# Wide attention: scores from query weights multiplied into the keys, values folded pass by pass

## The reference

```
query = layernorm(x)                              # (8, 256, 128)
q = (query @ Wq + bq).reshape(b, sq, 16, 64)      # Wq: 128 x 1024
k = (key @ Wk + bk).reshape(b, 64, 16, 64)        # key = value = context
v = (value @ Wv + bv).reshape(b, 64, 16, 64)
scores = einsum('bqhd,bkhd->bhqk', q, k) / 8
attn = softmax(scores, axis=-1)
out = einsum('bhqk,bkhd->bqhd', attn, v).reshape(b, sq, 1024)
out = out @ Wo + bo + query
return layernorm(out) * ln_gamma + ln_beta
```

## Time and profile before

| what | us |
|---|---|
| median of 3 runs | 1546.37 (1543.95 to 1548.54) |
| profiled execution, own time | 1538.79 |
| its span, first to last instruction | 1537.1 |
| PE busy in the span | 1341.4 (87%) |
| DVE, ACT, POOL busy | 1054.2 (69%), 936.5 (61%), 878.9 (57%) |
| mean granted TensorE clock, share of full | 0.941 |

### The profile page before, as it was taken

How to read it: one execution, slowest core, us unless ns; L and a number is a source line. 1 busy time by engine, 2 the same in 40 slices (tenths; PEclk the granted TensorE clock), 3 DMA queues, 4 the chain that set the end, 5 groups by cost and what they waited for, 6 DMA issues and landing times. The chain is left out here.

```text
span 1537.1 us, 25078 instructions
## 1 busy us (share of the span) xinstructions
PE 1341.4 (87%) x8116; PEld 1040.6 (68%) x8116; DVE 1054.2 (69%) x2126; ACT 936.5 (61%) x1435; POOL 878.9 (57%) x619
## 2 busy tenths in 40 slices
PE   9789999797888887789489999998898349999998
PEld 8767777465466666646368887885787338787786
DVE  5534444597699999889756666673666766666665
ACT  4467787553787876477246765556665327555554
POOL 4168888300899999532047776661345128666655
PEclk9689999898899999899689999999999769999999
DMA  6021110000000000030044435332000135443442
GB/s 250 1 63 43 42 48 27 2 2 1 1 1 1 1 0 0 26 142 2 1 136 127 127 123 178 129 124 113 2 1 1 55 78 130 122 130 123 129 120 86
DMA packets 51561, 103.31 MB, mean 67 GB/s; under 512 B 6248, under 2 KB 10928, under 8 KB 49936
## 3 DMA queue, kind: packets, MB, share of 16 engines
q1 hardware_dynamic: 51472, 102.17, 21.6%
HBM read 99.99 MB, written 2.16 MB: 66 GB/s over the span
## 5 line engine op out<-in xcount | busy, mean ns | idle before, releaser
L1541 POOL TENSOR_TENSOR RA<-RW 128x1024 f32<-128x1024 f32 x128 | 246.7, 1965 | 86.1 <-ACT RW L1502 86.1
L881 ACT ACTIVATE PS<-PS 128x512 f32<-128x512 f32 (+1 forms) x260 | 151.1, 582 | 215.3 <-PE PS L677 214.6
L974 POOL TENSOR_TENSOR l3f_hid_rest<-RW,l3f_hid_high 128x512 fp32r<-128x512 f32 x132 | 170.5, 1292 | 141.3 <-ACT l3f_hid_high L873 141.3
L974 POOL TENSOR_TENSOR l2f_hid_rest<-RW,l2f_hid_high 128x512 fp32r<-128x512 f32 x128 | 165.3, 1292 | 136.9 <-ACT l2f_hid_high L873 136.9
L974 POOL TENSOR_TENSOR l0f_hid_rest<-RW,l0f_hid_high 128x512 fp32r<-128x512 f32 x128 | 165.2, 1292 | 64.7 <-ACT l0f_hid_high L873 56.4
L934 DVE TENSOR_TENSOR RW<-RW,PS 128x512 f32<-128x512 f32 (+1 forms) x260 | 178.7, 687 | 11.7 <-DVE RW L929 0.9
L1572 PE MATMUL PS<-identf,RA 128*128 128x128 f32 x1024 | 139.8, 287 | 37.0 <-DVE RA L1463 33.1
L1572 PEld LDWEIGHTS PS<-identf,RA 128*128 128x128 f32 x1024 | 118.1, 147 | 72.6 <-DVE RA L1463 69.3
L1463 DVE SCALAR_TENSOR_TENSOR RA<-RA,RW,PS 128x1024 f32<-128x1024 f32 x128 | 157.0, 1277 | 11.0 <-ACT PS L1508 10.4
L1508 ACT ACTIVATE PS<-RA 128x1024 f32<-128x1024 f32 x128 | 130.1, 1026 | 54.3 <-DVE RA L1463 51.8
L934 DVE TENSOR_TENSOR RW<-RD,PS 128x512 f32<-128x512 f32 x128 | 87.9, 687 | 108.3 <-ACT PS L881 99.9
(11 more groups left out here) (339 smaller groups left out, 3346.4 us busy)
## 6 DMA issues: line engine op xcount, KB each, us to landing
RD<-l2f_kept SPq DMA_DIRECT2D x128, 256.0 KB, 3.5
RB<-l3f_kept SPq DMA_DIRECT2D x128, 256.0 KB, 3.7
RD<-l0f_kept SPq DMA_DIRECT2D x32, 256.0 KB, 3.1
RA<-in_w SPq DMA_DIRECT2D x2, 2048.0 KB, 10.0
RA<-in_wg SPq DMA_DIRECT2D x2, 1024.0 KB, 9.7
RA<-in_wu SPq DMA_DIRECT2D x2, 1024.0 KB, 11.7
RA<-in_wd SPq DMA_DIRECT2D x2, 1024.0 KB, 13.6
RC<-in_wg SPq DMA_DIRECT2D x1, 2048.0 KB, 8.5
```

Source lines behind the costliest of these rows:

```text
L881: act.activation(gate, gate, e.func, bias=st.bias).then_inc(e.acted, 1)
L974: pool.tensor_tensor(rest, hid, high, ALU.subtract).then_inc(e.hidden_ready, 1)
L1541: pool.tensor_tensor(*pair_scores(r, h), ALU.add).then_inc(added, 1)
```

## The change

Queries are no longer made. Since a score is `(x Wq + bq) . k`, the query weights of a head are multiplied into its keys once: `M = Wq k`, 128 features by 64 context tokens for each head and batch, kept in `MK` (half of it in the place of `KT`, half where `QT` was). A score is then the product of `XT` and `M`. For the bias: a row of the layer norm sums to zero over its features, so feature 0 is minus the sum of the others. DVE subtracts column 0 of the query weights from the other columns and puts the bias `bq` in column 0 (`fold_queries`), and ACT stores `XT` with its row 0 set to the constant 1 (scale `rest`, bias from the identity's first column). The array `wq3` is laid out transposed on the host, with the same size.

The value products move behind the first scores. The folds become halves of a batch (`fold(n)`, 8 products instead of 16), of which two are made ahead of the loop and one in each of its first 14 passes. A fold writes the first 256 columns of banks 4 and 5, which are the banks of the turned weights too; ACT stores every fold (1850). The outputs use banks 6 and 7 in turn.

The core of the diff, without the declarations of semaphores:

```diff
+    VW_unit = RB[:, 8192:16384].rearrange("p (b h i f) -> p b i h f", b=B, h=2, i=2)
+    MK = [RA[:, 4096:8192].rearrange("p (c n) -> p c n", c=8), KT]
+    vw_ps, out_ps = PS[:, TURN:TURN + 2, 0:2 * D], [PS[:, OUT + r, 0:D] for r in range(2)]
...
         def _(dve):
+            def fold_queries():
+                dve.wait_ge(k.l3x_loaded, 64)
+                own.settle(dve.tensor_tensor(wq[:, :, 1:D], wq[:, :, 1:D], over(wq[:, :, 0], 2, D - 1),
+                                             ALU.subtract))
...
+                dve.tensor_copy(wq[:, :, 0], k.cols[:, at:at + 8]).then_inc(folded, 1)
+                dve.tensor_scalar(rest, k.identf[:, 0:1], -1.0, 1.0, ALU.mult, ALU.add).then_inc(rest_made, 1)
+            norm_vector(dve, k, nm, own, between=fold_queries)
+            for c in range(8):
+                dve.wait_ge(m_ready, c + 1)
+                dve.tensor_copy(MK[1][:, c, :], PS[:, 3 + 2 * (c % 2), :]).then_inc(m_stored[1], 1)
...
-                if t < 2:
-                    for b in ((1,), (3, 5, 7))[t]:
-                        dve.wait_ge(vw_ready, b + 1)
-                        dve.tensor_copy(VW[:, b].rearrange("p j d -> p (j d)"), vw_ps[1]).then_inc(vw_stored[1], 1)
...
         def _(act):
+            def store_m(c):
+                act.wait_ge(m_ready, c + 1)
+                act.activation(MK[0][:, c, :], PS[:, 2 + 2 * (c % 2), :], ACT.Copy).then_inc(m_stored[0], 1)
...
-                act.activation(k.XT[:, bass.ts(q, BLK)], PS[:, q, :], ACT.Copy).then_inc(nm.xt_ready, 1)
+                act.activation(k.XT[:, bass.ts(q, BLK)], PS[:, q, :], ACT.Identity, bias=k.identf[:, 0:1],
+                               scale=rest).then_inc(nm.xt_ready, 1)
...
+            for c in range(8):
+                store_v(c)
+                if c == 3:
                     exp(0)
             exp(1)
-            for j in range(JOBS):
-                store_q(1, j)
+            for n in range(2):
+                store_vw(n)
...
             for t in range(NT):
-                if t // 2 + 2 < B:
-                    for j in (2 * (t % 2), 2 * (t % 2) + 1):
-                        store_q(t // 2 + 2, j)
+                if t + 2 < 2 * B:
+                    store_vw(t + 2)
                 act.wait_ge(p_turned, t + 1)
...
         def _(pe):
+            def query_keys(c):
+                pe.wait_ge(k_stored, c + 1)
...
+                for h in range(2):
+                    rows = slice(64 * h, 64 * h + 64)
+                    mm = pe.matmul(PS[:, 2 + 2 * (c % 2) + h, :], wq[rows, c, :], KT[rows, c, :], start=True, stop=True)
+                mm.then_inc(m_ready, 1)
...
             def scores(t):
...
+                for h in range(2):
+                    mm = pe.matmul(score[t % 2][:, bass.ts(h, BLK)], k.XT[:, bass.ts(t, P)],
+                                   MK[h][:, :, bass.ts(t // 2, C)], start=True, stop=True)
...
+            def fold(n):
+                b, i = n // 2, n % 2
+                if n >= 1:
+                    pe.wait_ge(vw_stored, n)
+                if n >= 3:
+                    pe.wait_ge(p_stored, n - 2)
+                for jj in range(2):
                     for h in range(2):
                         for half in range(2):
...
             def output(t):
                 pe.wait_ge(p_stored, t + 1)
-                if t >= 1:
-                    pe.wait_ge(out_added, t)
+                if t >= 2:
+                    pe.wait_ge(out_added, t - 1)
...
+            pe.wait_ge(nm.xt_ready, 2)
+            scores(0)
             pe.wait_ge(nm.xt_ready, NB)
-            fold(0)
-            scores(0)
             scores(1)
...
+            for c in range(8):
+                value(c)
+            pe.wait_ge(v_stored, 8)
+            for n in range(2):
+                fold(n)
             for t in range(NT):
+                if t + 2 < 2 * B:
+                    fold(t + 2)
                 if t + 2 < NT:
                     scores(t + 2)
...
+                pe.wait_ge(vw_stored, min(t + 3, 2 * B))
                 turn(t)
```

More of the change, by code:

```diff
@@ L1815, in _, with store_v, store_vw @@
                                bias=k.col("bk3", c)).then_inc(k_stored, 1)
+                if c >= 1:
+                    store_m(c - 1)
+            store_m(7)
+            act.wait_ge(rest_made, 1)
             for q in range(NB):
                 act.wait_ge(nm.xt_turned, q + 1)
-                act.activation(k.XT[:, bass.ts(q, BLK)], PS[:, q, :], ACT.Copy).then_inc(nm.xt_ready, 1)
[L1820 to L1825, removed]
+                act.activation(k.XT[:, bass.ts(q, BLK)], PS[:, q, :], ACT.Identity, bias=k.identf[:, 0:1],
+                               scale=rest).then_inc(nm.xt_ready, 1)
+            def store_v(c):
+                act.wait_ge(v_ready, c + 1)
+                act.activation(VT[:, c, :], PS[:, 4 + c % 4, :], ACT.Identity,
+                               bias=k.col("bv3", c)).then_inc(v_stored, 1)
+            def store_vw(n):
+                act.wait_ge(vw_ready, n + 1)
+                act.activation(VW_unit[:, n // 2, n % 2], vw_ps, ACT.Copy).then_inc(vw_stored, 1)
             def exp(t):
@@ L1870, in _ @@
             pe.wait_ge(k.l3x_loaded, 64)
+            def query_keys(c):
+                pe.wait_ge(k_stored, c + 1)
+                if c == 0:
+                    pe.wait_ge(folded, 1)
+                if c >= 2:
+                    for m in range(2):
+                        pe.wait_ge(m_stored[m], c - 1)
+                for h in range(2):
+                    rows = slice(64 * h, 64 * h + 64)
+                    mm = pe.matmul(PS[:, 2 + 2 * (c % 2) + h, :], wq[rows, c, :], KT[rows, c, :], start=True, stop=True)
+                mm.then_inc(m_ready, 1)
             for c in range(8):
-                if c >= 2:
-                    pe.wait_ge(v_stored, c - 1)
-                pe.matmul(PS[:, 4 + c % 2, :], wv[:, c, :], k.ctxT[:], start=True, stop=True).then_inc(v_ready, 1)
                 if c >= 2:
@@ L1877, in _ @@
                 pe.matmul(PS[:, 6 + c % 2, :], wk[:, c, :], k.ctxT[:], start=True, stop=True).then_inc(k_ready, 1)
-            norm_tensor(pe, k, nm)
[L1880 to L1890, removed]
+                if c >= 1:
+                    query_keys(c - 1)
@@ L1892, in scores @@
+            query_keys(7)
+            for m in range(2):
+                pe.wait_ge(m_stored[m], 7)
+            norm_tensor(pe, k, nm)
             def scores(t):
-                b = t // 2
                 if t >= 2:
                     pe.wait_ge(shifted, t - 1)
[L1896 to L1902, removed]
@@ L1903, in scores, with value @@
-                mm.then_inc(score_ready, 1)
[L1905 to L1908, removed]
+                for h in range(2):
+                    mm = pe.matmul(score[t % 2][:, bass.ts(h, BLK)], k.XT[:, bass.ts(t, P)],
+                                   MK[h][:, :, bass.ts(t // 2, C)], start=True, stop=True)
+                mm.then_inc(score_ready, 1)
+            def value(c):
+                if c >= 4:
+                    pe.wait_ge(v_stored, c - 3)
+                pe.matmul(PS[:, 4 + c % 4, :], wv[:, c, :], k.ctxT[:], start=True, stop=True).then_inc(v_ready, 1)
```

58 lines of the change are left out of this document (18 added, 40 removed).

## The result

| | median | of | ratio to before, 95% interval |
|---|---|---|---|
| before | 1544.26 us | 14 runs, beside the changed kernel | |
| changed kernel | 1537.96 us | 14 runs | 0.9965 [0.9948, 0.9982] |

The medians lie 6.3 us apart; the ratio puts the gain at 0.35%, 5.4 us. One execution of the changed kernel took 4479.22 us, and the ratio, which goes by the fast runs alone, leaves it out. Forecast were 1539.9 us, and 6.5 us of gain.

What follows compares the result with a forecast made beforehand. TensorE was taken to bound projections and loop, the chain over other engines the last 15 us. -6.3 (keys' +2.8 included) - 1.4 + 1.2 = -6.5 us on 1546.37 gave 1539.9 us, range 1534.4 to 1546.5.

Steps and rivals of the forecast that it cites:

- Keys: Keys' stretch, first product to transposes: 14 changes between 128-row and 64-row products at about 0.20 us, +2.8 us.
- rival 4: Keys' stretch: the two 64-row products of a pair don't overlap; +6.9 us, 1546.8 us, chance 0.06.
- To turn(2): First product to turn(2): queries and most folds go, values move behind scores; -6.3 us, the keys' 2.8 included.
- Loop: turn(2) to turn(13): queries go, a fold and its wait come; eleven periods 72.05 against 73.45 us, -1.4 us.
- the forecast's 6.50: Loop period by PE's row: turn 0.93, outputs to copy 2.05, copy to fold 1.07, fold 0.60, scores 1.85.
- the 6.55 by ACT's line: Loop period if turn waits for ACT's fold store behind copy, exp and splits: 0.93 + 2.05 + 3.57 us.
- Rivals 2 and 3: 2: free form changes, sooner fold store, about -12 us, chance 0.10; 3: whole-cost fold, period 7.02, -1.3 us, chance 0.18.
- rivals 5 and 6: 5: weight loads by the column, dearer fold, about -4 us, chance 0.03; 6: fold products don't overlap, +11.4 us, chance 0.08.
- the -4 that the prediction names: Whole sum if weight loads took columns / 1.2 ns: about -4 us instead of -6.5.
- End: turn(13) to the last outputs' start: 14.15 us instead of 12.92, the old loop's overlap missing; +1.2 us.
- Sum: Whole stage: -6.3 - 1.4 + 1.2 = -6.5 us.
- Time: Whole kernel: 1539.9 us, on the median 1546.37 of the runs shown; chance 0.55.

Runs made afterwards that it cites:

- The experiment above: Changed kernel plus 12 idle products on PE ahead of turn(14): 1538.63 us; turn(13) to last outputs 14.31 us, against 15.88 without.

## Why the prediction was right, and where it was not

- **Keys**, +2.8: right, and for the reason given. The transposes started 19.25 us behind the first product, 19.5 was forecast; fourteen changes at 0.20 are 2.8, and the start at 1.2 GHz, which the forecast left as it was, came out shorter by the rest. The pair of 0.86 rules out rival 4. The Trainium skill (TensorEngine Tiling (Array Packing), Tiling Modes) has it that a change of tiling mode drains TensorE; it gives no price. This trace agrees that a change costs time, 0.20 us each; what that time goes into it doesn't show.
- **To turn(2)**, -6.3: turn(0) stood 18.86 us behind the transposes (18.85 forecast), turn(1) 6.18 behind it (6.05), turn(2) 6.53 (6.55). From the first product to turn(2) it is 50.82 against 57.33 us: -6.5. The wait was the forecast's too: turn(1) started 0.10 us behind the end of POOL's normalising, the end of the softmax chain, though the profile names ACT's store. Of the 128 fold products ahead of turn(0), 24 are left there, so 104 are gone, and not 96.
- **Loop**, -1.4: 71.58 against 73.45 us, -1.9. Period 6.51 by PE's row: turn 0.88, outputs to copy 2.04, copy to fold 1.17, fold 0.60, scores 1.82. That was the forecast's 6.50, whose terms miss by up to 0.10 and cancel; the 6.55 by ACT's line that I used instead lay 0.17 short of deciding (the store ends at 1108.36 and turn starts at 1108.56). Rivals 2 and 3 fell with it, and rivals 5 and 6 with the fold's 0.60. For the fold the Trainium skill's load rule (TensorE: Matmul & The Clock Gate, LDWEIGHTS) would have given 0.85, an estimate; the trace doesn't agree. By that rule the forecast's own sums would have come to about -2.4, an estimate too (0.28 more in each of eleven passes, 0.33 in each of three folds ahead), and not to the -4 that the prediction names.
- **End**, +1.2: +2.96. This is the step that failed, by size: I took turn and outputs at the loop's lengths, and behind 3.36 us of idle PE they ran at half the clock. The experiment above puts 1.57 of the 1.73 us missed on that.
- **Sum**: -6.5 - 1.9 + 3.0 = -5.4 in the stage, against -6.5. The loop gained 0.5 more than forecast and the end cost 1.7 more, so in part they cancel.
- **Time**: 1539.9 stood on a median of three runs, 1546.37; the fourteen gave 1544.26, 2.1 less. So most of the 1.9 us between forecast and result lies in that base, and not in the change.

Why the profiled pair shows only -0.7: the stage's -5.42 stands beside two differences from code that wasn't touched. The layers ahead took 3.07 us longer (first product at 1051.23 instead of 1048.16). And the next layer's last group of gates ran at 1.2 GHz; timeline of PE, before and then after:

```profile
1217.70 2.00 PE L1017 MATMUL PS<-gates,XT 128*128 128x64 f32 x16
```

```profile
1215.36 3.52 PE L1017 MATMUL PS<-gates,XT 128*128 128x64 f32 x16
```

That is +1.5, together -0.8. Neither is shown to come from the change: the same group took 1.96 or 1.97 us in two of the other runs without idle products at that place, and 3.5 in the rest.

## What to carry to other kernels

Taking work off the busiest engine is worth only what the next wait leaves: look at which buffer the new work shares, with whom, and what stood in the gap that the removed work covered. Here 14 us of products left the loop for 1.9 us of time; two free pieces of psum and the order of three lines were worth another 17. And a time summed from rows at 2.4 GHz holds only where the clock stays up: here one idle stretch of 3.36 us let it fall, and so did a row of short ones, told below. And an experiment that takes one cost away can bring the next wait to light: ask which store would set the pace before reading a price from it.

## What was not expected of the hardware

- The granted clock differs between executions in places where nothing was changed; what decides it isn't shown. One group of the product-keys layer, timeline of PE, before and then after (mean granted clock over it 0.75 and 0.50):

```profile
368.90 4.79 PE L1549 MATMUL PS<-RC 128*128 128x32 f32 x32 [1.26 <-PEq L1153]
```

```profile
369.54 7.00 PE L1549 MATMUL PS<-RC 128*128 128x32 f32 x32 [1.26 <-PEq L1153]
```

  Over the twelve profiled executions, that work being the same in all, it took 4.8 to 5.2 us in six and 7.0 in six. In the first six the stage's first product came at 1046.6 to 1048.4 us, in the others at 1051.2 to 1054.4. So these 2.2 us may be part of what makes the runs of one kernel differ too; that, and the rest, no run here shows.
- The clock fell in a row of short gaps as well as in a long one: behind folds of 0.67 us with 0.72 us idle ahead of each, a fold then took 1.13, and the mean granted clock of the 23 us up to the next scores was 0.50. Gaps of 2.25 or 2.26 us ahead of turn(14) left the clock up in two runs; in two others it fell just behind that turn, and the outputs took 3.34 and 3.42 us instead of 1.95.
